# A two-block preactivation convolution: its lead rebuilt, with statistics exchanged through memory, the normalizing moved to ScalarE, and the 5x5 code run once on zeros

## What is computed

```python
x = x + conv3x3(_gn(x), masked weight)      # _gn: G=16 groups, mean and variance over 2 x 128 x 128
x = x + conv5x5(_gn(x), kernel) + bias      # the FFT form of the reference is a 5x5 convolution, padding 2
# the 3x3 weight is masked where its mean magnitude over the outputs is not above the threshold
# (and the mask falls back to score > 0 where no more than 1% would be kept)
```

## Time and profile before

| | us |
|---|---|
| median of 3 runs | 880.9 |
| the profiled execution | 882.4 |
| its span, first to last instruction | 880.6 |
| TensorE busy | 789.2 (90%) |
| VectorE busy | 679.1 (77%) |
| ScalarE busy | 326.0 (37%) |
| GpSimd busy | 317.3 (36%) |
| mean granted TensorE clock | 0.964 of full |

### The profile page before, as it was taken

How to read it: one execution, slowest core, us unless ns; L and a number is a source line. 1 busy time by engine, 2 the same in 40 slices (tenths; PEclk the granted TensorE clock), 3 DMA queues, 4 the chain that set the end, 5 groups by cost and what they waited for, 6 DMA issues and landing times.

```text
span 880.6 us, 108990 instructions
## 1 busy us (share of the span) xinstructions
PE 789.2 (90%) x52300; PEld 705.5 (80%) x52300; DVE 679.1 (77%) x989; ACT 326.0 (37%) x417; POOL 317.3 (36%) x154
## 2 busy tenths in 40 slices
PE   1673579999999999999999999999999999998884
PEld 1552368888989889899888888988989889987773
DVE  5576378979898989989897989898998878664210
ACT  0122024344344444344434434444434443433331
POOL 1020004444433333334434444333334444443332
PEclk9887789999999999999999999999999999999998
DMA  8954965969787787868696868878795556454222
GB/s 178 211 120 116 221 153 135 234 144 225 172 215 201 198 207 188 218 168 223 151 236 144 221 178 206 211 196 208 182 220 157 158 147 160 107 136 114 66 56 56
DMA packets 83843, 150.52 MB, mean 171 GB/s; under 512 B 20960, under 2 KB 28384, under 8 KB 79712
## 3 DMA queue, kind: packets, MB, share of 16 engines
q1 hardware_dynamic: 79200, 145.92, 67.7%
q10 hardware_dynamic: 4608, 4.23, 1.9%
HBM read 75.60 MB, written 33.59 MB: 124 GB/s over the span
## 4 chain that ended last, share of the span: by engine, by line
PE 77%; DVE 10%; issue 4%; SPq 3%; DMA 2%; ACTq 1%; ACT 1%; DVEq 1%; POOL 0%; POOLq 0%
PE psum L711 76%; DVE x L572 3%; SPq L225 2%; DMA x_bands<-x_dram 2%; DVE bn_in L498 1%; DVE x_bands L557 1%; ACTq L398 1%; DVE bn_out L600 1%; DVE mid L592 1%; DVEq L595 1%; DVE mid_bands L557 1%; SPq L220 0%; DVE product L530 0%; POOL mid L322 0%; DVE deviation L534 0%
## 5 line engine op out<-in xcount | busy, mean ns | idle before, releaser
L322 POOL TENSOR_TENSOR mid<-mid,conv_out 128x512 f32<-128x512 f32 x128 | 308.0, 2437 | 502.4 <-ACT conv_out L355 489.1
L711 PE MATMUL psum<-x_hi,s 32*32 32x512 f16 x25600 | 378.0, 382 | 21.4 <-issue 9.7
L711 PEld LDWEIGHTS psum<-x_hi,s 32*32 32x32 f16 x25600 | 343.0, 88 | 47.3 <-issue 16.6
L711 PE MATMUL psum<-x,s 32*32 32x512 f16 x13824 | 228.9, 391 | 28.0 <-DVEq L595 14.7
L711 PEld LDWEIGHTS psum<-x,s 32*32 32x32 f16 x13824 | 176.4, 88 | 78.9 <-issue 49.2
L711 PE MATMUL psum<-x_lo,s_hi 32*32 32x512 f16 x12800 | 186.1, 376 | 3.5 <-issue 3.3
L711 PEld LDWEIGHTS psum<-x_lo,s_hi 32*32 32x32 f16 x12800 | 175.8, 88 | 8.4 <-issue 4.6
L580 DVE TENSOR_TENSOR x_lo<-mid_bands,x_hi 128x2560 f16<-128x2560 f32 x32 | 102.3, 3197 | 59.4 <-PE psum L711 59.0
L572 DVE TENSOR_TENSOR x<-x_bands,x 128x2304 f16<-128x2304 f32 x32 | 100.6, 3144 | 35.2 <-PE psum L711 35.2
L355 ACT ACTIVATE conv_out<-psum,bias,unscale 128x512 f32<-128x512 f32 x128 | 94.4, 769 | 60.1 <-PE psum L711 60.0
L364 ACT ACTIVATE s<-s_lo 128x800 f16<-128x800 f16 x32 | 27.9, 871 | 179.3 <-PE psum L711 179.3
(11 more groups left out here) (74 smaller groups left out, 175.1 us busy)
## 6 DMA issues: line engine op xcount, KB each, us to landing
x_own<-x_dram SPq DMA_DIRECT2D x128, 256.0 KB
mid_bands<-mid SPq DMA_DIRECT2D x512, 64.0 KB
out_dram<-mid SPq DMA_DIRECT2D x128, 256.0 KB
x_bands<-x_dram SPq DMA_DIRECT2D x96, 288.0 KB, 6.1
x_bands<-x_dram SPq DMA_DIRECT2D x32, 272.0 KB, 7.4
mid_bands<-mid SPq DMA_DIRECT2D x224, 32.0 KB
every_mv<-mv_scratch ACTq DMA_DIRECT2D x16, 256.0 KB
w<-L_conv_kernel_dram SPq DMA_DIRECT2D x4, 100.0 KB, 18.6
```

The lines of the kernel that those rows point to most:

```text
L322: nc.gpsimd.tensor_tensor(m, m, conv_out[:, b, :], ALU.add).then_inc(out_added, 1)
L711: ins = nc.tensor.matmul(psum[quad(j), bank + i, :].rearrange("p (a w) -> p a w", a=A), w[quad(i), at, :], src[quad(i), A * j + dy:A * (j ...
```

## The change

The changes, in eight groups:

1. **Zeros ahead.** VectorE first clears `x5_hi` and `s5` and grants one token of `w5_go`. TensorE then does four matmuls on them and jumps into the loop's `inner5` (384 matmuls of the 5x5 code, on zeros), leaves it through two new labels at the loop's end, and only then begins its lead.
2. **Statistics.** x of image 1 and mid of image 0 go through memory as well (exchanges 1 and 2); only x of image 0 still goes through TensorE. The sums over partitions for the weights (`over_partitions`) move from TensorE to VectorE: a broadcast, a 32 x 32 transpose and a reduction.
3. **Normalizing** moves from VectorE to ScalarE in all steps, save half 0. VectorE makes one more value per statistic for it (`gshift`).
4. **Edges first.** `move_edges` is split by direction, and in the steady steps it comes ahead of `move_mid`. In the lead `load_bands(5)` is issued before the first move and `load_own(3)` earlier.
5. **The lead on TensorE** has `keep_warm(9)` after the second pass and again at the end of each of its steps, and 18 instead of 11 before the first. The first two passes of step 3 run in the lead's copy.
6. ScalarE's order in the lead is written out apart; in the steady steps `normalize(0, s + 1)` stands ahead of the low 5x5 weights and `normalize(1, ...)` ahead of the high ones.
7. VectorE's order of steps 0 to 3 is written out apart: the 5x5 weights' bound in step 0, `low3(3)` ahead of `low5(0)`.
8. GpSimd and `high5(0)` wait until the zeros have been used (`a5_inner`).

```diff
@@ sync
-            def move_edges(n):
+            def move_edges(n, source, to):
+                sp.wait_ge(mid_made, PIECES * (2 * n + source + 1))
...
             load_bands(4)
+            load_bands(5)
             move_mid(0)
             load_own(2)
+            move_edges(0, 1, 0)
             move_mid(1)
-            move_edges(0)
-            load_bands(5)
+            load_own(3)
+            move_edges(0, 0, 1)
             load_bands(6)
-            load_own(3)
+            load_bands(7)
             move_mid(2)
...
                 if has3(s):
+                    if s % 2:
+                        move_edges(s // 2, 1, 0)
+                        move_edges(s // 2, 0, 1)
                     move_mid(s)
-                    if s % 2:
-                        move_edges(s // 2)
@@ scalar
+            def normalize(which, h):
+                t, slots, landed, each, made = ((x_bands, XB_SLOTS, x_bands_in, Q, scaled1),
+                                                (mid_bands, MB_SLOTS, mid_bands_in, MOVES, scaled2))[which]
+                act.wait_ge(landed[h % slots], 16 * each * (h // slots + 1))
+                act.wait_ge(scale_ready, ROOTS.index((("x", "mid")[which], h // 2)) + 1)
+                v, at = t[:, h % slots, :, :], slice(which, which + 1)
+                nc.scalar.activation(v, v, ACT.Identity, bias=gshift[:, at], scale=gscale[:, at]).then_inc(made, 1)
...
+            for s in range(LAG):
+                act.wait_ge(c3_early, 3 * s + 1)
+                weights3(s3_lo, 0, 1)
+                act.wait_ge(c3_inner, 3 * s + 1)
+                weights3(s3_lo, 1, 1)
+                if s == 0:
+                    spread_stats(X1_EXCHANGE)
+                if s == 1:
+                    take_root(("x", 1))
+                if s == 2:
+                    spread_stats(MID0_EXCHANGE)
+                act.wait_ge(c3_whole, 2 * s + 1)
+                weights3(s3_hi, 0, 2)
+                weights3(s3_hi, 1, 2)
+                if s == 0:
+                    normalize(0, 1)
+                    gather_stats(X1_EXCHANGE)
+                if s == 1:
+                    normalize(0, 2)
+                if s == 2:
+                    gather_stats(MID0_EXCHANGE)
+                    normalize(0, 3)
+                high3(s + 1)
+                if s == 2:
+                    take_root(("mid", 0))
+                    normalize(1, 0)
+                    high5(0)
@@ vector
+            nc.vector.memset(x5_hi[:, :, :], 0.0)
+            nc.vector.memset(s5[:, :, :], 0.0).then_inc(w5_go, 1)
...
+            def over_partitions(to, src):
+                own_step(nc.vector.tensor_scalar(across[:, :], ones[:, 0:C], src, None, ALU.mult))
+                own_step(nc.vector.transpose(turned[:, :], across[:, :]))
+                own_step(nc.vector.tensor_reduce(to, turned[:, :], AX.X, ALU.add))
@@ tensor
-            pe.reg_mov(visit5, 0)
-            pe.br("lead_first3")
+            pe.reg_mov(visit5, ALONE)
+            pe.wait_ge(w5_go, 1)
+            for b in range(BANKS):
+                nc.tensor.matmul(psum[:, X5_BANK + b, :], s5[:, 0:Q, :].rearrange("p t o -> p (t o)"),
+                                 x5_hi[:, 0:A, 2:2 + W], start=True, stop=True)
+            pe.br("begin")
+            with nc.body("begin", valid_engines=only):
+                pe.br_eq(visit5, ALONE, on_true="hot", on_false="lead")
+            with nc.body("lead", valid_engines=only):
...
+                mix_mean(("x", 0))
+                mix_variance(("x", 0))
+                keep_warm(18)
...
-            pe.br("first3")
+            pe.br("inner5")
...
             with nc.body("no3", valid_engines=only):
-                pe.br_eq(visit5, ALONE + 1, on_true="inner5", on_false="last5")
+                pe.br_eq(visit5, ALONE + 1, on_true="alone", on_false="last5")
...
+            with nc.body("alone", valid_engines=only):
+                pe.br_eq(step, 0, on_true="begin", on_false="second5")
+            with nc.body("second5", valid_engines=only):
+                pe.br("inner5")
```

More of the change, by code:

```diff
@@ L381, in _ @@
             high3(0)
-            for s in range(STEPS + 1):
+            for s in range(LAG):
[25 more added lines that the diff above has]
+                    high5(0)
+            for s in range(LAG, STEPS + 1):
                 gathered = exchanged(s - 1)
@@ L411, in _ @@
                     take_root(gathered[0])
-                if s == 2:
-                    take_root(("mid", 0))
+                if s == LAG:
+                    take_root(("x", 2))
+                    normalize(0, s + 1)
                 if has3(s + 1):
                     high3(s + 1)
-                if s == 0:
-                    take_root(("x", 1))
+                if has5(s + 1):
+                    normalize(1, s + 1 - LAG)
                 if has5(s):
@@ L550, in scale_of, with clear_pad @@
                                                          ALU.mult, ALU.mult))
-            def normalize(which, h):
-                t, slots, landed, each = ((x_bands, XB_SLOTS, x_bands_in, Q), (mid_bands, MB_SLOTS, mid_bands_in, MOVES))[which]
-                dve.wait_ge(landed[h % slots], 16 * each * (h // slots + 1))
-                v = t[:, h % slots, :, :]
-                nc.vector.tensor_scalar(v, v, gmean[:, which:which + 1], gscale[:, which:which + 1],
-                                        ALU.subtract, ALU.mult).then_inc(scaled, 1)
-            def clear_pad(which, h, done):
-                dve.wait_ge(scaled, done)
-                t, slots, counted = ((x_bands, XB_SLOTS, norm1), (mid_bands, MB_SLOTS, norm2))[which]
+                nc.vector.scalar_tensor_tensor(gshift[:, at], gmean[:, at], -1.0, gscale[:, at],
+                                               ALU.mult, ALU.mult).then_inc(scale_ready, 1)
+            def clear_pad(which, h):
+                t, slots, made, counted = ((x_bands, XB_SLOTS, scaled1, norm1), (mid_bands, MB_SLOTS, scaled2, norm2))[which]
+                dve.wait_ge(made, h + which)
                 q, at = pad_rows(h % 2, which + 1)
@@ L682, in _ @@
                     take_conv3(s)
-                if has5(s + 1) and not s % 2:
-                    normalize5(s + 1 - LAG)
                 if has3(s):
                     stats_out(s)
-                if s == LAG:
-                    stats_in(7, range(BANKS))
+                if has5(s + 1):
+                    clear_pad(1, s + 1 - LAG)
                 if exchanged(s):
@@ L701, in _ @@
         def _(pe):
-            def over_partitions(bank, src):
-                nc.tensor.matmul(psum[:, bank, 0:1], ones[:, :], src, start=True, stop=True).then_inc(w_summed, 1)
             def tap(w, at, src, t, k, bank, start=False):
@@ L884, in _ @@
                 pe.reg_add(visit5, visit5, ALONE)
-                pe.br_lt(step, STEPS, on_true="first5", on_false="all_done")
+                pe.br_lt(step, STEPS, on_true="first5", on_false="leave")
+            with nc.body("leave", valid_engines=only):
+                pe.br("all_done")
+            with nc.body("alone", valid_engines=only):
+                pe.br_eq(step, 0, on_true="begin", on_false="second5")
+            with nc.body("second5", valid_engines=only):
+                pe.br("inner5")
             nc.switch_bb("all_done")
```

216 lines of the change are left out of this document (105 added, 111 removed).

## The result

The changed kernel takes 939.85 us (median of 4 runs, 933.67 to 946.21), the kernel before 880.68 in the same comparison: ratio 1.067, 95% interval 1.058 to 1.077. It is slower by 59 us; 870.7 us was forecast, and the range ended at 890. The profiled execution took 934.99 us with a span of 933.2, so 52.6 us of span are to be found.

The account below looks back on a forecast made before the run. TensorE fills the steady steps, so the stretch ahead of step 4, with its waits and code fetches, was left to gain; +21.1 for the zeros and -31.3 for the lead gave -10.2 us: 870.7 us, range 853 to 890.

Parts of the forecast that it names:

- The way in: TensorE's jump to the zeros' code: the first piece comes at light load, 3.3 + 3.6 = 6.9 us.
- the upper bound: Zeros ahead of the first mix: all pieces at 8.78 us give a mix at 49.1, +29.2 us.
- The first 3x3: Sign in TensorE's timeline: the first 3x3 at 48.6 us, after the first mix at 41.
- The pieces behind: Further pieces of `inner5` in the zeros' run: three at 8.0 us each under full DMA, reaching 30.9 us.
- The way out: Leaving the zeros through `alone` at the loop's end: a fifth piece, from 32.8 to 40.8 us.
- The pieces of `inner5` are there: Step 3: the 5x5 code is already fetched, so stalls of 4.41 and 5.26 us go; step 31 us, -20.8.
- Rival C: Newer pieces displace the zeros' code if only about eight fit; step 3 fetches again: 889 us, chance 0.20.
- The lead's steps 0 to 2: Steps 0 and 1 take 13.5 us each (-5.5, -0.3), step 2 takes 16.7 us (-4.8).
- Rival A: Zeros' code comes quickly, but image 1's exchange falls under full DMA, 19.4 us: 862 us, chance 0.20.
- The steady steps: From step 4 on: ScalarE's 4.4 us more per step is hidden, steps stay 23.8 us; cost 0, between -3 and +20.
- D: Rival: ScalarE becomes late in the steady steps, 0.7 us a step, +19.6: 890 us, chance 0.05.
- The last steps: The last 79.9 us, behind step 31: normalizing lies in a gap of ScalarE, change 0.

Follow-up runs that it names:

- e3: The changed kernel with a first branch straight to `inner5` and the way out of the zeros beside the 5x5 code: 916.56 us, ratio 1.038.
- e2: The changed kernel without the zeros' run and with the loop entered at its first label `first3` in step 3: 876.59 us, ratio 0.996.
- e1: The changed kernel without the zeros' run, the loop still entered at `inner5`: 904.20 us, ratio 1.025.
- e6: e3 with 2 warming matmuls in each place instead of 18 and 9, so a shorter lead: 918.81 us, 1 run.
- e9: e3 with the zeros' run moved to the end of step 2, followed by a jump back for step 3: 920.84 us, 1 run.
- e10: e7 with `move_mid` ahead of `move_edges` again in steps 3 to 31: 870.61 us, ratio 0.989.
- e7: e2 with the loads of halves 4 and 5 held back until the exchange of image 1 has landed: 869.67 us, ratio 0.986.
- e4: The changed kernel with the loads of x held back until the zeros are through: 923.94 us, 1 run.
- e5: The kernel before without the hint on its loop's closing branch: 1455.07 us, one run, against 882.46 before.

## Why the prediction was wrong

The forecast erred by 62.8 us on the profiled execution. By its own steps:

*The way in: counted as one piece, was three.* "The first comes at light load: 3.3 + 3.6 = 6.9 us." With one branch that is right (7.74 in e3), but the changed kernel came to 23.70. The program showed the branch through `hot` to the loop's start and from there to `inner5`, and this was not followed. +16.8 us; even the upper bound, a mix at 49.1, fell 11.6 us short. (The first 3x3 was due at 48.4 by the forecast's own sum, not at 48.6.)

*The pieces behind.* Forecast 8.0 us each, measured 8.57, 8.85 and 9.31 between the stalls' ends: +2.7. The way out 8.4 and not 8.0, but with four packets from 51 to 58.3 us and nearly idle DMA engines (share 0.05 from 49 to 60.74), so that here the sum was met by chance. For the pieces the reading of the earlier trace rows was sound; with the way in it makes the 19.9 us by which the mix at 40.8 was missed.

*"The pieces of `inner5` are there": the step that failed.* It assumed that code once fetched stays, whatever TensorE does between. The earlier trace rows say only that the loop, entered at its start and closed by a hinted branch, stays. Step 3 took 62.4 us and not 31, step 4 40.35 and not 23.8: +47.9 us together. Two things make up this sum. Even e2, which enters at `first3` and has no zeros, takes 71.8 us for the two steps where 54.8 were forecast: 17.0 us, since the stalls that the zeros were to remove (9.7 us ahead of the pieces on x_hi, 5.8 in the low image) are simply there, and the clock of the step is 0.77 of full. The other 30.9 us belong to a term that the forecast put at nothing without a reason: step 3 now goes through the lead's copy and enters the loop in its middle. e1 against e2 gives 30.6 for it (27.6 by medians): 14.0 in step 3, and 16.6 in step 4, most likely for the hint that was not passed.

*Rival C* had the right place and the right sign for step 3, with 889 us. Its cause, displacement of the zeros' code by newer pieces, is refuted by e6 and e9, and its price (3.6 + 4 x 1.7, at light load) was too small: the DMA share was 0.88 and the clock 0.64 of full from 112 to 149 us, and step 4 had stalls again. No run shows its condition, that there is room for only about eight pieces. What the runs show is that code was fetched again with fewer packets in between, five in e6 (8 to 103 us) and five in e9 (79.5 to 105). Its sign, 14 packets or more, came as 30.

*The lead's steps 0 to 2: right.* 13.05, 13.97 and 16.73 us against 13.5, 13.5 and 16.7. The exchange met a free DMA (share 0.16 from 71.49 to 81.42 us). ScalarE's transfers and VectorE's first use of them after the change:

```profile
71.49 0.35 ACTq L390 DMA_DIRECT2D mv_scratch<-mv  x1
73.31 0.33 ACTq L395 DMA_DIRECT2D every_mv<-mv_scratch  x1
```

```profile
81.42 0.60 DVE L593 SCALAR_TENSOR_TENSOR product<-every_mv,mix 128x128 f32<-128x128 f32 x1 [0.21 <-issue]
```

9.9 us from the write to the use, and nobody waited, so the exchange itself, forecast at 7, took at most that. But this gain was the zeros' own doing: they had let the loads finish; e1, without them (share 1.05 from 31 to 52 us), took 55.4 us for these three steps and not 43.75. *Rival A* priced the other case, and e1 and e2 show it: 31.05 to 52.29 in e2 is 21.2 us (19.4 by its rows), with 9.19 us of TensorE waiting there and 9.57 in e1.

*The steady steps: right, D refuted.* 641.29 / 27 = 23.75 us a step against 23.84 before. ScalarE's new passes, from the page:

```profile
L353 ACT ACTIVATE mid_bands<-mid_bands,gshift,gscale 128x2560 f32<-128x2560 f32 x32 | 80.5, 2517 | 2.5 <-DVE gshift L614 2.5
L353 ACT ACTIVATE x_bands<-x_bands,gshift,gscale 128x2304 f32<-128x2304 f32 x31 | 71.6, 2311 | 2.1 <-DVE gshift L614 1.3
```

2.52 + 2.31 = 4.8 us a step where 4.4 was forecast, all of it in idle time. Where the 0.1 us a step comes from is not settled; e10 excludes the order of the edges.

*The last steps* gained 2.9 us: the first pass over x_hi took 7.0 to 7.4 us, partly at a lower clock (0.86 of full from 805 to 812 us before), in all three of the 5x5-only steps before and in one after (5.7 to 5.8 in the other two). That differs between executions and is not put down to the change.

Sum: 19.9 + 47.9 + 0.1 for steps 0 to 2 - 2.4 - 2.9 = 62.6, against 62.8 measured. The profiled execution lies 4.9 us below the median of the changed kernel; that part is not in any trace read here.

## What to carry to other kernels

Running code on dummy data to have it at hand pays only if it stays, and here not one stall was saved by it; ask for a row that shows code kept across the very jumps that the kernel makes. Count for every jump all the pieces that its branches pass through (three here, 19.10 us), at the price of the DMA load at that moment, and enter a loop so that the place of its branch hint is passed before the first closing branch (e2 against e1: 27.6 us less). Free a small transfer on the critical path by holding a large load back (e7: 14.4 us from write to use and not the 21.2 of e2), not by delaying everything.

## What the runs showed of the hardware

- A packet of code was 16 KB, and 126 to 128 matmuls lay between two stalls of a pass (the changed kernel, step 3). From stall end to stall end a piece cost 8.6 to 9.3 us under full DMA (the changed kernel, share 0.96 from 23.7 to 50.4 us). With the DMA engines free (share 0.02), the stalls between pieces were 0.5 to 1.8 us (e4).
- A loop whose closing branch had no hint fetched nine packets a pass, and the kernel took 1455 us against 882 (e5).
- A loop that stayed after entry at its start, where its hint is (e2: one packet from 131 us on), was fetched again in its second pass after entry in its middle, past the hint (e1 against e2: 19 packets against 10, 27.6 us). The nine packets and the 40.2 us of that pass are those of a pass without a hint (e5: nine, 40.56 us).
- Code left by a jump back was fetched again at the next entry (stalls of 20.3 us in e3, 17.7 in e6, 15.97 in e9), even where that jump itself found its target at hand (0.84 us, e9).
- An exchange of statistics through memory took 21.2 us from write to use under loads that were issued early (e2, DMA share 1.05), 14.4 us at most at a share of 0.71 (e7), and at most 9.9 us at a share of 0.16 (the changed kernel).
